# Block 0 of a fused attention and FP4 feed-forward kernel: reciprocal roots iterated on GpSimd, and seven quads' token biases added by VectorE

## The reference

```python
def _layernorm(x, axis=-1, eps=1e-05):
    m = jnp.mean(x, axis=axis, keepdims=True)
    v = jnp.var(x, axis=axis, keepdims=True)
    return (x - m) / jnp.sqrt(v + eps)
...
txt_proj = jnp.einsum('btd,de->bte', textual_features, Ws)
feat_proj = jnp.einsum('bfd,de->bfe', features, W)
h = jnp.tanh(txt_proj[:, None, :, :] + feat_proj[:, :, None, :] + b[None, None, :, :][..., 0, :])
rho = jnp.einsum('bftd,d->bft', h, w[:, 0])
...
w_s = jnp.tanh(jnp.einsum('bfd,od->bfo', txt_h, Wcw) + bcw)
b_s = jnp.tanh(jnp.einsum('bfd,od->bfo', txt_h, Wcb) + bcb)
return w_s * features + b_s
...
gate = fp4_linear(x, w_gate)
y = fp4_linear(x, w_up)
h = jax.nn.silu(gate) * y
return fp4_linear(h, w_down)
...
x = x + _L0_xattn_ref(_layernorm(x, axis=-1), ...)
x = x + _L0_ffn_ref(_layernorm(x, axis=-1), ...)
```

## Time and profile before

| | |
|---|---|
| median of 3 runs | 1555.12 us |
| lowest and highest run | 1552.08, 1555.3 us |
| the profiled execution, its own time | 1555.08 us |
| its span | 1553.3 us |
| busy over the span: PE, ACT, DVE, POOL | 93%, 88%, 76%, 16% |
| span covered by block 0 up to the drain of its scores | to 360.86 us |

### The profile page before, as it was taken

The page is one execution under the profiler, slowest core; times in us unless marked ns, Lnnn a source line. Parts: engine busy times, 40 slices in busy tenths (PEclk is TensorE's granted clock), DMA queues, the critical chain, the costliest instruction groups (busy, mean ns, idle before and its releaser), DMA issues.

```text
span 1553.3 us, 24405 instructions
## 1 busy us (share of the span) xinstructions
PE 1441.6 (93%) x9752; PEld 649.6 (42%) x9752; DVE 1182.5 (76%) x1974; ACT 1363.3 (88%) x1265; POOL 245.8 (16%) x412
## 2 busy tenths in 40 slices
PE   6989999866989999999999999989999999989998
PEld 4334444411333333343444444434444444545554
DVE  6499999864486667749776767698877787898887
ACT  4999999999999999999999999999999999433331
POOL 1032222210020101101111111011111111112211
PEclk9999999988999999999999999999999999999999
DMA  4133333330011111102111111112111111123332
GB/s 144 35 77 82 83 83 83 83 64 28 15 26 40 27 40 40 20 24 50 40 40 40 35 32 40 40 27 53 40 40 40 40 40 40 40 55 77 78 68 62
DMA packets 180823, 77.91 MB, mean 50 GB/s; under 512 B 163916, under 2 KB 163916, under 8 KB 180710
## 3 DMA queue, kind: packets, MB, share of 16 engines
q1 hardware_dynamic: 180016, 75.00, 21.2%
q10 hardware_dynamic: 693, 1.36, 0.3%
HBM read 27.85 MB, written 8.39 MB: 23 GB/s over the span
## 4 chain that ended last, share of the span: by engine, by line
PE 58%; ACT 20%; DVE 19%; issue 1%; DMA 1%; POOL 0%; SPq 0%; ACTq 0%; DVEq 0%; POOLq 0%
PE rho L756 21%; ACT hring L580 12%; PE dn L848 11%; PE gu0g L834 6%; PE gu0u L834 5%; PE gu1g L834 5%; PE gu1u L834 5%; ACT hring L575 4%; DVE work L959 2%; ACT featT L580 1%; DVE sm L945 1%; DVE work L977 1%; DVE work L978 1%; ACT featT L575 1%; DVE featT L925 1%
## 5 line engine op out<-in xcount | busy, mean ns | idle before, releaser
L580 ACT ACTIVATE hring<-featT,bias 128x1024 f32<-128x1024 f32 x724 | 766.6, 1151 | 12.7 <-PE rho L756 12.7
L756 PE MATMUL rho<-hring,wslide 128*32 128x512 f32 x3840 | 468.5, 613 | 60.9 <-ACT hring L580 53.7
L756 PEld LDWEIGHTS rho<-hring,wslide 128*32 128x32 f32 x3840 | 108.0, 111 | 340.9 <-issue 199.1
L848 PE MATMUL dn<-wd_room,turned 128*128 128x512 f16 x1023 | 230.6, 379 | 1.1 <-DMA turned<-work 1.0
L575 ACT ACTIVATE hring<-featT 128x4096 f32<-128x4096 f32 x57 | 207.4, 3638 | 0.7 <-DVE featT L925 0.6
L473 POOL TENSOR_SCALAR split_t<-sm 128x88 f32<-128x88 f32 (+3 forms) x93 | 22.8, 245 | 1159.0 <-DVE sm L948 1158.9
L580 ACT ACTIVATE featT<-featT,bias 128x1024 f32<-128x1024 f32 x180 | 193.4, 1180 | 0.0
L925 DVE TENSOR_SCALAR featT<-featT,bias 128x1024 f32<-128x1024 f32 x256 | 175.5, 750 | 10.0 <-ACT hring L575 6.3
L1226 DVE TENSOR_TENSOR work<-sg,gu1u 128x352 f32<-128x352 f32 x64 | 33.3, 521 | 167.2 <-ACT sg L613 166.2
L848 PEld LDWEIGHTS dn<-wd_room,turned 128*128 128x128 f16 x1023 | 96.5, 98 | 146.1 <-issue 36.0
L834 PE MATMUL gu0g<-wg,turned 128*128 128x352 f16 x768 | 126.0, 314 | 5.2 <-DMA turned<-xq 3.2
(11 more groups left out here) (192 smaller groups left out, 1628.9 us busy)
## 6 DMA issues: line engine op xcount, KB each, us to landing
xt<-in_x SPq DMA_DIRECT2D x32, 256.0 KB, 2.9
out<-xt SPq DMA_DIRECT2D x32, 256.0 KB, 2.4
work<-in_x SPq DMA_DIRECT2D x10, 512.0 KB, 3.9
xt<-in_x SPq DMA_DIRECT2D x6, 512.0 KB, 4.0
xt<-in_L_ffn_w_gate SPq DMA_DIRECT2D x11, 256.0 KB, 2.7
xt<-in_L_ffn_w_up SPq DMA_DIRECT2D x11, 256.0 KB, 2.7
work<-in_L_ffn_w_down SPq DMA_DIRECT2D x2, 704.0 KB, 4.3
xt<-in_L_ffn_w_down SPq DMA_DIRECT2D x2, 704.0 KB, 4.4
```

Source lines behind the costliest of these rows:

```text
L580: act.activation(slot[s][:, g, :], featT[:, e, ROW0[k]:ROW0[k] + rows], ACT.Tanh, bias=bias[:, e, base + tok:base + tok + 1]).then_inc(tan ...
L756: last = pe.matmul(rho[SLOTW * g:SLOTW * g + SLOTW, hf * 512:hf * 512 + 512], wslide[:, e, SLOTW - 1 - r:2 * SLOTW - 1 - r], slot[s][:, g, ...
L848: last = pe.matmul(dn[:, :], hqT[:, a, c, :], wd[:, bb, c, :], start=(c == 0 and i == 0), stop=(c == NC - 1 and i == 2))
```

## The change

Two things are moved, both in block 0.

First, the Newton steps of the pairs go from VectorE to GpSimd. `stats_pair` keeps three instructions behind the statistics: variance plus epsilon, the shift, the seed. `normalise_pair` on GpSimd begins with the negated mean and three times four instructions on 128 x 2, each waiting for the one before it, and then scales the pair as before. This holds for all twelve pairs.

Second, seven quads of block 0 (18, 23, 27, 32, 36, 41, 45: `HEAD_SUMS`) become summed quads. Their sums go to the last block's columns of `featT`. VectorE makes them in passes 1 to 7, right after `copy_pair(w)` (`head_sum`, four instructions of 128 x 1024). In the same passes `stats_pair(w + 1)` is put ahead of `gate_up_weights(w + 1, 0)`, and on GpSimd `normalise_pair` ahead of the `split` that serves those gate weights. In pass 9 VectorE waits for quad 45 before it writes features of the last block. Rooms and quads of the later blocks stay as they are.

```diff
+    LAST_BLOCK = NBLK - 1
...
+    HEAD_SUMS = [14 + 9 * w // 2 for w in range(1, 8)]
+    for i, m in enumerate(HEAD_SUMS):
+        summed_quads.append(m)
+        room_of[m], room_from[m] = LAST_BLOCK, HEAD_SUMS[i - 1] if i > 0 else None
...
                 pool.wait_ge(pair_stats, p + 1)
                 t0 = HEAD_T + 2 * p
+                y, v, h = rstd[:, t0:t0 + 2], pair_var[:, 0, :], pair_var[:, 1, :]
+                small(pool.tensor_scalar(nmean[:], stat[:, t0:t0 + 2, 0:1].rearrange("p t a -> p (t a)"), -1.0, 1.0,
+                                         ALU.mult, ALU.mult))
+                for i in range(3):
+                    small(pool.tensor_tensor(h, y, y, ALU.mult))
+                    small(pool.tensor_tensor(h, h, v, ALU.mult))
+                    small(pool.tensor_scalar(h, h, -0.5, 1.5, ALU.mult, ALU.add))
+                    small(pool.tensor_tensor(y, y, h, ALU.mult))
...
             for w in range(1, NC):
-                split(D)
-                normalise_pair(w)
+                if 1 <= w - 1 <= len(HEAD_SUMS):
+                    normalise_pair(w)
+                    split(D)
+                else:
+                    split(D)
+                    normalise_pair(w)
                 split(D)
...
+            def head_sum():
+
+                n = summed_quads[sums[0]]
+                if room_from[n] is None:
+                    dve.wait_ge(first_ready, 1)
+                else:
+                    dve.wait_ge(tanh_ready, GRP * (room_from[n] + 1))
+                to = ROW0[LAST_BLOCK]
+                for g in range(GRP):
+                    r, e = quad_at(n)
+                    dve.tensor_scalar(featT[:, g, to:to + BLOCKS[0]], featT[:, e, 0:BLOCKS[0]],
+                                      bias[:, e, GRP * r + g:GRP * r + g + 1], None, ALU.add).then_inc(summed, 1)
+                sums[0] += 1
...
-                step(ts(nmean[:], stat[:, t0:t0 + 2, 0:1].rearrange("p t a -> p (t a)"), -1.0, None, ALU.mult))
-                signal(rsqrt(rstd[:, t0:t0 + 2], stat[:, t0:t0 + 2, 1:2].rearrange("p t a -> p (t a)"), 2, last=True),
-                       pair_stats, p + 1)
+                step(ts(pair_var[:, 0, :], stat[:, t0:t0 + 2, 1:2].rearrange("p t a -> p (t a)"), EPS, None, ALU.add))
+                step(ts(pair_var[:, 1, :].bitcast(I32), pair_var[:, 0, :].bitcast(I32), 1, None, ALU.logical_shift_right))
+                signal(ts(rstd[:, t0:t0 + 2].bitcast(I32), pair_var[:, 1, :].bitcast(I32), -1.0, float(RSQRT_SEED),
+                          ALU.mult, ALU.add), pair_stats, p + 1)
...
             for w in range(NC - 1):
                 copy_pair(w)
-                gate_up_weights(w + 1, 0)
-                stats_pair(w + 1)
+                if 1 <= w <= len(HEAD_SUMS):
+                    head_sum()
+                    stats_pair(w + 1)
+                    gate_up_weights(w + 1, 0)
+                else:
+                    gate_up_weights(w + 1, 0)
+                    stats_pair(w + 1)
+                if w == len(HEAD_SUMS) + 2:
+                    dve.wait_ge(tanh_ready, GRP * (HEAD_SUMS[-1] + 1))
                 if w > 0:
                     features_pair(w - 1)
                 gate_up_weights(w + 1, 1)
```

More of the change, by code:

```diff
@@ L108, in bass_xattn_fp4_ffn @@
     summed_quads, room_of, room_from = [], {}, {}
+    LAST_BLOCK = NBLK - 1
     SUMS = {1: range(12, QPB, 3), 2: [3, *range(11, QPB, 4)], 3: [2, 5, *range(11, QPB, 3)]}
+    HEAD_SUMS = [14 + 9 * w // 2 for w in range(1, 8)]
+    for i, m in enumerate(HEAD_SUMS):
+        summed_quads.append(m)
+        room_of[m], room_from[m] = LAST_BLOCK, HEAD_SUMS[i - 1] if i > 0 else None
     last_in = {r: QPB * (r + 1) - 1 for r in range(NBLK)}
+    OTHERS = len(HEAD_SUMS)
     for k in range(1, NBLK):
@@ L113, in bass_xattn_fp4_ffn @@
             m = QPB * k + q
-            room = 0 if k == 1 else 1 + len(summed_quads) % (k - 1)
+            room = 0 if k == 1 else 1 + (len(summed_quads) - OTHERS) % (k - 1)
             room_of[m], room_from[m] = room, last_in[room]
@@ L193, in bass_xattn_fp4_ffn @@
         minus = sb("minus", [P, 8])
+        pair_var = sb("pair_var", [P, 2, 2])
         top_minus = sb("top_minus", [P, 8])
```

## The result

The changed kernel takes **1595.08 us** (median of 4 runs, 1592.97 to 1595.42) against 1554.37 us for the kernel before (4 runs): a ratio of 1.0261, 95% interval 1.0249 to 1.0273, 40.7 us slower. The profiled execution took 1595.27 us, 1.8 us more than its span, as before.

A forecast was written before the change was run, and what follows sets the result against it. VectorE's pass was taken to bound block 0 up to about 260 us: 19.34 + 2.66 - 1.97 + 0.95 + 3.95 = 24.9 us, seven passes +39, with the others +43, so 1598 us. Range 1590 to 1604 (0.70).

The forecast's parts named there:

- The sums: VectorE, passes 1 to 7: four sums add 2.66 us a pass, with no wait for the previous summed quad's tanh.
- The small instructions off VectorE: VectorE, passes 1 to 7: ten of thirteen small instructions leave, -1.97 us a pass; 0.61 stay.
- The wait for the load: Passes 1 to 7: statistics could start 4.11 us into the pass, the load lands at 5.04; VectorE waits +0.95 us.
- The wait for the split: Passes 1 to 7: GpSimd, held up by VectorE, ends the split 9.0 us after the seed; VectorE waits +3.95 us.
- The other passes: Block 0: pass 0 +2.0 us, passes 8 and 9 split about 1.3 late, -0.7 each; pair 9's transposes 43 to 44 later.
- From pair 9 to the end: Pair 9's transposes to block 0's end: 117.5 us at ScalarE's pace, unchanged, so the shift stays +43 us.
- ScalarE's 4.5 us: ScalarE, block 0: seven summed quads save 0.65 us each, worth nothing, since ScalarE will wait about 6 us a pass.
- A: GpSimd's small instructions not held up by VectorE: split wait 1.7 us, pass 22.7, 1580 us; chance 0.13.
- B: Split in passes 1 to 7 hidden altogether: pass 21.0 us, +12 in all, 1567 us; chance 0.05.
- C: ScalarE sets block 0's pace, so the 4.5 us saved reach the end: faster, 1545 to 1550 us; chance 0.05.
- E: VectorE's sums wait for ScalarE, adding only beyond the load's 0.95 us; time as forecast, counted in its 0.70.
- D: Hold-up works both ways, or GpSimd's small instructions take 0.35 us: 1 us more a pass, 1606 us; chance 0.06.

The follow-up runs named there:

- the sums alone: Kernel before plus seven summed quads in block 0, without the reordering and with Newton steps on VectorE: 1572.9 us, ratio 1.0124.
- Newton back: Changed kernel with the negated mean and Newton steps back on VectorE, sums and orders as changed: 1580.35 us, ratio 1.0173.
- the split first: Changed kernel with GpSimd making the gate weights' split ahead of Newton steps and scalings in all passes: 1572.36 us, ratio 1.0122.
- the early load: Changed kernel with SyncE issuing the next pair's load ahead of the transposing transfer of the pass before: 1586.47 us, ratio 1.021.
- split first and early load together: Changed kernel with GpSimd's split ahead of the Newton steps and the pair's load ahead of the transfer: 1565.84 us, ratio 1.0075.
- six steps: Changed kernel with six Newton steps on GpSimd for three, twelve more small instructions in each pair: 1630.42 us, ratio 1.0489.

## Why the prediction was right

**What bounds block 0.** VectorE's pass, read from a chain without gaps. Sums alone made it 2.62 us longer, and in each run with the seven sums the drain came later by what pair 9's transposes came later, to within 2 us (25.8 for 27.6 with Newton back, 18.9 for 18.3 with the sums alone, 18.3 for 20.3, 32.0 for 31.2 and 11.5 for 11.8 with the split first, the early load and both), only with six steps by 6 us more (76.0 for 69.9). In these and the changed kernel ScalarE is busy for the same 281.2 to 282.3 us from 70 us to the drain, while the drain lies between 372 and 437.

**The sums**, +2.66: measured 2.74 with the overlap, and 22.0 for the pass that held nothing else new. Right.

**The small instructions off VectorE**, -1.97: three remain, from 150.65 to 151.26, 0.61. Right.

**The wait for the load**, +0.95: 0.85 to 1.81, 8.2 us in seven passes, 1.17 each, and its removal gave 8.1. Right in kind, and 1.5 us short in all; the waits of the last two passes are 1.51 and 1.81.

**The wait for the split**, +3.95: measured 3.37. Two terms were mis-sized. The hold-up: I let five small instructions pass ahead of VectorE's product, held five and let three run free, T + 5.9. Six passed ahead (the sixth at 152.77, 0.04 before the product), two shared one instruction of VectorE (153.91 and 154.19, 0.19 and 0.24 us), four were held (153.04, 154.51, 154.98, 155.72), and only one ran free: through 5.4 us after the seed (156.64 - 151.23). And the four instructions of a free split take 1.2 us (158.36 to 159.57), not 1.47: I had taken L475's 373 ns, which was for 88 columns.

**The pass**, 24.9: 24.47 here, 24.68 on the mean of six (99.74 to 247.80), so 5.3 more than before and not 5.6. Seven make 37. That this is so near the forecast is in part two errors against each other: the split 0.6 us too dear, the load 0.2 too cheap.

**The other passes.** Pass 0: the wait was 3.37, so +1.4 for +2.0. Pass 8: 0.87 for 1.3. Pair 9's transposes came 39.9 us late, for 43 to 44: its statistics began 37.4 us late (274.47 against 237.05) and not 41, which is the passes and pass 0, and GpSimd's chain from there to the transposes was 2.5 us longer for 2.7.

**From pair 9 to the end**, 117.5 us and no change: 401.00 - 283.14 = 117.9. Right, and so is VectorE's end, still 10.55 us ahead of its last wait; I had it 13 ahead, since the drain came 3 us earlier than I thought.

**ScalarE's 4.5 us**, worth nothing: right, by all runs with seven sums. From 70 us to the drain it idles 48.9 us for 6.2, 42.7 more, 6.1 for each of the seven passes, as forecast; its busy time falls from 284.7 to 282.1, 2.6 us and not 4.5.

**The rivals.** A (no hold-up, 1580) lies inside my range, and what excludes it is not the time but the rows of GpSimd and the wait of 3.37 for its 1.7. B falls with the same wait, C with the sums alone. E isn't seen: no sum in the changed kernel has idle time ahead of it. D's second half, the lock that works both ways, exists (the Trainium skill, "SBUF — State Buffer", section on who interferes with whom: whoever issues first holds the shared pair), but doesn't bite in the changed kernel, where GpSimd's scalings run while VectorE stands still. It bites where the order lets both run: 0.3 us a pass with split first.

## What to carry to other kernels

Where one engine's serial list sets the pace, moving work off it can cost more than it gains if the engine that takes it over is the one it waits for later in the same round; place the answer it needs first (here a split of 1.2 us; 21.8 us by its place alone) ahead of work that only the next round needs. Hoisting a step also hoists the need for its data: look at which queue, behind which transfer, its load is issued. And work moved onto the pacing engine cost its full duration here, 2.66 us for each 0.65 that it saved an engine that was 99% busy.

## What the runs showed of the hardware

The exclusion between VectorE and GpSimd works both ways, the half that I had left out of the sum: under a GpSimd scaling of 128 x 512 VectorE's instruction of 128 x 32 took 0.35 us for 0.18, and its 128 x 512 one 0.59 for 0.43. The kernel before has it too, in pass 0, where GpSimd's scalings run from 88.20 to 89.73:

```profile
89.42 0.34 DVE L950 TENSOR_SCALAR sm<-sm 128x32 f32<-128x32 f32 x1
```

So the trace on which the forecast rests could have priced it. How long a small GpSimd instruction is held is how much of VectorE's is left when it starts, to within 0.1 us: 0.78 us where it starts 0.23 into a product of 1.09, 0.65 and 0.64 early in a `tensor_tensor` of 0.69, 0.39 and 0.24 later in a `tensor_scalar` of 0.43 and 0.45, and 0.19 where it came 0.03 us first. Not held are those beside VectorE's reduction of 128 x 512 and its copies out of PSUM; with split first and early load together eight in a row, from 149.03 to 151.15, take 0.19 us each while VectorE copies and reduces. The cost of thirteen instructions, 5.25 us, is thus no property of them: twelve more, run while VectorE stood still, cost 3.28.

After long waits TensorE was slow for a while: in the changed kernel all eight waits of 4.03 to 8.55 us for a pair are followed by transposes of 1.11 or 1.12 us, where those of pair 9 took 0.66 before. The length of the wait alone doesn't decide it: with Newton back one of 4.13 us was followed by 0.66 (198.54). Behind a wait of 2.91 us, in the kernel before, the transposes took 0.66 but the quad behind them was as slow as the one in the changed kernel, 3.42 us for 3.37, where others took 1.9:

```profile
244.28 3.42 PE L756 MATMUL rho<-wd_room,wslide 128*32 128x512 f32 x16
```

The granted clock, a mean of the two levels 2.4 and 1.2 GHz, was 0.86 in 150 to 250 us, where the earlier trace rows had 0.97 and 0.90. In these passes no cost of it is seen: TensorE came to each pair from 133.98 to 283.14 early and waited at least 4.03 us, and from pair 9 to the drain it is 117.9 us for 117.6.
